# Reordering the node stages between the edge passes of a four-layer graph network: factors before tables, turns before products, a bias added by groups

## The reference, cut to what matters

```python
h = maximum(layernorm(x), 0);  x = x + L0(h)   # attention, W1, batch norm, relu, W2 (+ b2)
h = maximum(layernorm(x), 0);  x = x + L1(h)   # q,k,v = h @ W + b; softmax per target; agg @ Wo + bo
h = maximum(layernorm(x), 0);  x = x + L2(h)   # h @ W, softmax per target of leaky scores
h = maximum(layernorm(x), 0);  x = x + L3(h)   # weighted sum over edges, two products, leaky relu
```

## Time and profile before

| what | value |
|---|---|
| median of 3 runs | 11529.81 us (11526.19 to 11531.22) |
| profiled execution, its own time | 11527.12 us |
| its span, first to last instruction | 11525.4 us |
| busy share of the span: POOL, DVE, ACT, PE | 71%, 63%, 47%, 9% |
| mean granted TensorE clock | 0.517 of full speed |
| stage j1, first product to last table | 4942.5 to 5067.9 us |
| stage j2, first scatter to the head of p2 | 7208.4 to 7289.8 us |

### The profile page before, as it was taken

One profiled execution on the slowest core, in us unless ns is written; L12 is line 12 of the kernel. 1 busy time (PEld: TensorE's weight loads), 2 busy tenths in 40 slices (PEclk: granted clock), 3 DMA queues, 4 the chain that ended last, 5 costly groups with the idle time before them and its releaser, 6 DMA issues.

```text
span 11525.4 us, 40086 instructions
## 1 busy us (share of the span) xinstructions
PE 1039.5 (9%) x4242; PEld 856.6 (7%) x4242; DVE 7232.6 (63%) x7083; ACT 5376.1 (47%) x6139; POOL 8189.6 (71%) x8632
## 2 busy tenths in 40 slices
PE   4122222221000000030000001100000000000001
PEld 3112222221000000020000000100000000000001
DVE  8845555553888888759999997445444543333333
ACT  6144444442666666546666665333333333333332
POOL 2177777777777777657777776777777767777776
PEclk8555555555555555565555555555555555555555
DMA  8756666663666666546666665333333333333333
GB/s 296 264 189 202 204 205 202 201 205 114 215 215 211 213 215 214 183 130 222 225 220 222 224 220 163 85 111 110 113 113 109 112 95 106 103 105 106 106 104 105
DMA packets 793528, 1946.33 MB, mean 169 GB/s; under 512 B 213957, under 2 KB 425885, under 8 KB 792860
## 3 DMA queue, kind: packets, MB, share of 16 engines
q1 hardware_dynamic: 461412, 1129.66, 27.4%
q0 software_dynamic: 331904, 814.65, 25.4%
HBM read 1204.91 MB, written 738.73 MB: 169 GB/s over the span
## 4 chain that ended last, share of the span: by engine, by line
POOL 49%; DVE 22%; issue 20%; DMA 4%; ACT 2%; PE 1%; another core or an unknown queue 1%; DVEq 0%; POOLq 0%; SPq 0%; ACTq 0%
POOL region L1353 47%; DVE work L1498 5%; DVE psB L1403 4%; DMA region<-x,ix_s 2%; DVE psR L1435 2%; DVE work L1431 2%; DVE psR L1491 2%; DVE psR L1483 2%; POOL work L1768 1%; DVE region L645 1%; DVE region L646 1%; PE psB L834 1%; DVE m_ext L1466 0%; POOL start_rows_by_dst L1125 0%
## 5 line engine op out<-in xcount | busy, mean ns | idle before, releaser
L1498 DVE TENSOR_TENSOR_SCAN work<-work,psR 128x1792 f32<-128x1792 f32 (+2 forms) x496 | 1971.1, 3974 | 92.1 <-DVE ix_s L1422 56.1
L1353 POOL DMA_INDIRECT region<-kv,ix_s x1612 | 1525.5, 946 | 497.0 <-issue 494.2
L1353 POOL DMA_INDIRECT region<-x,ix_s x1612 | 1520.9, 944 | 503.0 <-issue 459.6
L1353 POOL DMA_INDIRECT region<-qm,ix_s x1612 | 1523.4, 945 | 492.5 <-issue 489.4
L1353 POOL DMA_INDIRECT region<-h,ix_s x1612 | 1521.2, 944 | 491.3 <-issue 488.9
L1353 POOL DMA_INDIRECT region<-k,ix_s x1612 | 1521.0, 944 | 491.3 <-issue 491.3
L1516 ACT COPY work<-region 128x1664 f32<-128x1664 f32 (+1 forms) x496 | 1162.2, 2343 | 1266.6 <-DMA region<-start_rows_by_dst 735.0
L1403 DVE TENSOR_TENSOR_SCAN psB<-psB,work 128x1792 f32<-128x1792 f32 (+1 forms) x496 | 1485.0, 2994 | 387.1 <-ACT psB L1529 333.7
L1590 ACT COPY work<-work 128x1664 f32<-128x1664 f32 (+2 forms) x496 | 1539.2, 3103 | 0.0
L1589 ACT COPY psR<-work 128x128 f32<-128x128 f32 (+2 forms) x496 | 190.2, 384 | 2728.8 <-DVEq L1499 2728.8
L1431 DVE TENSOR_TENSOR work<-region,psB 128x1664 f32<-128x1664 f32 x372 | 702.1, 1887 | 801.2 <-DMA region<-k,ix_s 528.0
(11 more groups left out here) (330 smaller groups left out, 5060.1 us busy)
## 6 DMA issues: line engine op xcount, KB each, us to landing
region<-start_rows_by_dst SPq DMA_DIRECT2D x248, 832.0 KB, 6.7
state_p<-work SPq DMA_DIRECT2D x124, 936.0 KB, 4.8
state_p<-work SPq DMA_DIRECT2D x124, 884.0 KB, 3.8
region<-start_rows_by_src SPq DMA_DIRECT2D x124, 832.0 KB, 7.4
start_rows_by_dst<-zero_t SPq DMA_DIRECT2D x62, 1664.0 KB, 7.6
state_pA<-work SPq DMA_DIRECT2D x124, 832.0 KB, 4.9
state_p<-work SPq DMA_DIRECT2D x124, 832.0 KB, 3.5
start_rows_by_src<-zero_t SPq DMA_DIRECT2D x1, 59904.0 KB, 163.5
```

Source lines behind the costliest of these rows:

```text
L1353: g_.indirect_dma_start(rows_s[b][:, k, 0:wd_s], None, q.tabs, bass.IndirectOffsetOnAxis(ap=ix_s[b][:, k:k + 1], axis=0))\
L1498: c.do(nc.vector.tensor_tensor_scan(q.st[:, 0:F * (K + 1)], decay_at(q, b)[:, 0:F * (K + 1)], summed[:, 0:F * (K + 1)], 0.0, ALU.mult, ALU ...
```

## The change

In j1 and in j2 a group's factors are made ahead of the table of the group in front of it. PE transposes a group's normalised rows before the next group's W2 product (j1), and in j2 before the table product it also turns the values of the group two further on; `values` and ACT's copy of them run one group further ahead. `bo` is added group by group inside the loop of j1 and no longer at the start of p1.

```diff
-        def proj_pe(pe, nm, w, ncol, g):
+        def proj_turn_pe(pe, nm, g):
             pe.wait_ge(*proj_on(nm, "norm", g + 1))
             pe.wait_ge(*proj_on(nm, "ht", g + 1))
             for j in range(nb(g)):
                 ins = nc.tensor.transpose(psA[:, j * P:(j + 1) * P], hst[:, j, :], ident[:, :])
             ins.then_inc(S("proj_tr"), 1)
+
+        def proj_pe(pe, nm, w, ncol, g):
             pe.wait_ge(*proj_on(nm, "ht", g + 2))
...
-            if q is P1:
-                bias_dve(v, bo_1)
...
+            def group_bias(g):
+
+                xg = blocks(xsb, g)
+                c.do(nc.vector.tensor_tensor(xg, xg, bo_1[:, :].unsqueeze(1).to_broadcast([P, nb(g), D]), ALU.add))
+
             for g in range(NG):
                 add(g)
                 norm_dve(v, "j1", g)
+                factors_dve(v, "j1", g)
+                if g > 1:
+                    group_bias(g - 2)
                 if g:
                     take_dve(v, "j1", 3 * D, g - 1)
-                factors_dve(v, "j1", g)
+            group_bias(NG - 2)
             take_dve(v, "j1", 3 * D, NG - 1)
+            group_bias(NG - 1)
...
             for g in range(NG):
+                proj_turn_pe(pe, "j1", g)
                 if g < NG - 1:
                     second(g + 1)
                 proj_pe(pe, "j1", wcat1[:, :], 3 * D, g)
...
             values(0)
-            for g in range(NG):
-                if g < NG - 1:
-                    values(g + 1)
+            values(1)
+            for g in range(NG):
                 add(g)
                 norm_dve(v, "j2", g)
+                factors_dve(v, "j2", g)
+                if g < NG - 2:
+                    values(g + 2)
                 if g:
                     take_dve(v, "j2", D + 8, g - 1)
-                factors_dve(v, "j2", g)
             take_dve(v, "j2", D + 8, NG - 1)
...
-            def product(g):
+            def turn(g):
                 pe.wait_ge(S("e1_steps"), g * 3 + 3)
                 for j in range(nb(g)):
                     ins = nc.tensor.transpose(psD[:, j * P:(j + 1) * P], vals[:, j, :], ident[:, :])
                 ins.then_inc(S("end_tr"), 1)
+
+            def product(g):
                 pe.wait_ge(S("end_at"), g + 1)
...
+            turn(0)
             product(0)
+            turn(1)
             for g in range(NG):
                 if g < NG - 1:
                     product(g + 1)
+                proj_turn_pe(pe, "j2", g)
+                if g < NG - 2:
+                    turn(g + 2)
                 proj_pe(pe, "j2", w_2[:, :], D + 8, g)
...
             turned(0)
-            for g in range(NG):
-                if g < NG - 1:
-                    turned(g + 1)
+            turned(1)
+            for g in range(NG):
                 proj_act(act, "j2", g)
+                if g < NG - 2:
+                    turned(g + 2)
```

## The result

| | median us | lowest to highest | runs |
|---|---|---|---|
| before | 11526.65 | 11525.63 to 11531.22 | 5 |
| changed | **11467.96** | 11465.29 to 11469.76 | 5 |

The ratio is 0.9946 with an interval of 0.9935 to 0.9958: faster, by 58.7 us. The profiled execution of the changed kernel took 11469.12 us with a span of 11467.4.

The account below looks back on a forecast made before the run. POOL's queue was taken to bound the five passes, so gains lay in the node stages and pass starts: 11527.1 - 34.1 (j1) - 6.2 (bias) - 17.8 (j2) = 11469.0 us. Range given 11457 to 11491, its own 11461 to 11478.

Parts of the forecast that it names:

- The passes: Five passes: bound by POOL's queue, loops untouched; the end moves by whatever time a pass's first gather moves.
- j1, -34.1: Stage j1: period falls from 9.8 to 6.6 us a group, so p1's head gather is issued 34.1 us earlier.
- the ring: In j1: add, factors, normalisation, transposes, next W2 product, add set the period; 6.14 us at high clock, 7.65 low.
- nearer the high end: In j1: period taken as 6.6 us, closer to 6.14 at PE's higher clock level than to 7.65 at the lower.
- The head, -6.2: Start of p1: without DVE's one bias addition the first gather follows the head gather at once, saving 6.2 us.
- Held by something else: Rival at p1's start: not DVE's bias delays the head gather, which stays at 7.14 us; total 11475.2, chance 0.06.
- j2, -17.8: Stage j2: POOL scatters back to back, 5.1 us a group, so p2's head gather comes 17.8 us earlier.
- PE at the lower level, 5.65 us a group: In j2: PE's transposes, table product and Wo product at 1.2 GHz take 5.65 us a group, against POOL's 5.1.
- The signs named: Expected profile: j1 tables about 6.6 us apart, transposes right behind line 834, p1 head 0.98 us, j2 scatters at 1.275 us.
- TensorE at its lower level in j1: Rival in j1: PE stays at the lower clock, 7.65 us a group, gain only 22.7; total 11480.4, chance 0.14.
- the overlap that doesn't form: Rival in j1: transposes keep waiting on ACT or PE, only the bias gain remains; total 11521, chance 0.04.
- the lockstep of 13.4 us a group: Rival in j1: table product waits for the same turn's table, 13.4 us a group; total 11591, chance 0.03.

Follow-up runs that it names:

- the longer normalisation: Changed kernel with one more block of ACT normalisation per group in j1 and j2, into an unread tile: 11473.46 us.
- the longer product: Changed kernel with the table product of one block done twice per group in j1 and j2: 11461.29 us.
- PE's old order: Changed kernel with PE's next W2 product ahead of the transposes again in j1: 11470.69 us, ratio 0.9935.
- the one-input reduction: Changed kernel plus a DVE column sum of xsb with one SBUF input at p1's start, result unread: 11460.32 us, ratio 0.9942.

## Why the prediction was right, step by step

- **The passes**: p1 +0.2 us, the rest -2.4. Moving their first gather moved the end, as said.
- **j1, -34.1 against -36.6.** The mechanism stands: the ring is in the chain, the longer normalisation lengthened it, the longer product didn't. The period at the higher level is 6.19 us (6.14 forecast), at the lower 6.9 to 7.5 (7.65). From the end of the second W2 product to the end of the last, for which the sum has 71.9 us, it took 70.5 (ten periods of 6.50 on the mean and a short one of 5.5), 1.4 less. The last full product took 2.85 us and not the 4.6 taken, 1.75 less. Two small terms were left out: that product waits 0.45 us for ACT's copy, and POOL's part behind the last full table took 6.85 us and not 6.6. The two mis-sized terms are the clock's: "nearer the high end" was not near enough. The Trainium skill (TensorE: Matmul & The Clock Gate, What's actually happening) has the clock follow how busy PE was of late; the rise of 0.78 to 0.89, 1.00 with the longer product and 1.00 in PE's old order agree in direction. By that rule alone the time was to be 6 to 7 us below the sum; j1 came out 2.5 us below it.
- **What the prediction didn't ask**: whether PE's new order in j1 was any good. It found the W2 product in the ring and priced it, but held it only against other rings of the changed order and never against that of PE's order before, in which DVE's 5.27 us are the bound.
- **The head, -6.2 against -6.2.** Right, and shown by three kernels: gone without the addition, moved to the last scatter with it, absent beside the one-input reduction. "Held by something else" (0.06) is out. The Trainium skill (SBUF — State Buffer, Who interferes with whom) infers that a two-input tensor_tensor leaves the making of descriptors alone; 7.14 and 6.76 us against 0.98 and 0.97 say otherwise here. An indirect DMA of this kernel also takes its row numbers from an SBUF tile (`head_i`, `spos`), and no run separates that reading from the making of the descriptors. The bias in the loop is hidden only by slack: four scatters show 1.24 to 1.27 us beside it (one at 4999.88).
- **j2, -17.8 against -18.2.** POOL scattered back to back, as forecast: 61.45 us from the first to the last start, 48 x 1.275 being 61.2, and one scatter at 1.21 us where the sum allowed 1 us in all for such. The step "PE at the lower level, 5.65 us a group" was mis-sized: the clock was 0.72 over the stage, 0.76 in its middle, and no table waited for PE. It made no difference, since POOL was found to be the last either way. Against the old j2 of the other profiles the gain is 11 to 12 us. What the prediction got right is the length of the new stage, 63.5 us against 63.1, which repeats; the difference is near the mark only for the profile it was taken from.
- **The sum.** 11469.0 us against a median of 11467.96 is closer than the terms deserve: in the profiled execution the edited stretches gave 2.9 us more than forecast, and the ones that no edit touches took 3.1 us longer. That they cancel is luck.
- **The signs named.** The tables are 6.4 us apart, the head takes 0.98 us and stands 1.29 us ahead of the first gather, and POOL is idle for at most 0.31 us between two of j2's scatters. One sign was drawn wrongly: the transposes do not stand right behind the table product but wait for the normalisation (1.40, 2.01 and 1.13 us in three turns from 4995 on), as the ring asks.
- **The remaining rivals.** TensorE at its lower level in j1 (7.65 us a group) came in some groups, never in all. Neither the overlap that doesn't form nor the lockstep of 13.4 us a group left a trace.

## What to carry to other kernels

When a software pipeline is reordered, list for each engine's new order which product now stands in which ring, and price the old order of one engine beside the new order of another: here DVE's edit was worth 53 us (133.1 to 79.8 for j1, with the granted clock up from 0.73 to 0.89) and PE's in the same change gave 11 of them back. A long VectorE addition of two SBUF tensors should not stand where GpSimd issues indirect DMAs that the end hangs on; cut it to pieces and place them where GpSimd has slack. The stages whose ring ran through TensorE while its granted clock changed (0.54 to 0.71 over the old j2) had no fixed length (81.3, 75.4, 74.0 us): take the price of such a stage from several profiles before a gain is credited to an edit.

## What was not expected of the hardware

- More work on TensorE made the stage shorter: one product block more per group took the granted clock over j1 from 0.85 to 0.94 and j1 from 91.1 and 92.1 to 89.5 us. It is one profile, and the size is near the spread of j1 in kernels without it (90.1 to 92.2).
- An indirect DMA is held if it starts beside DVE's two-input addition, and by what is left of that: 6.16 us over its usual time with 6.29 to go, 5.7 with 5.83, 5.79 with 5.93. One that started 0.03 us behind the start of a group's addition (5019.17 in the changed kernel) was not held: 0.97 us. A one-input `tensor_scalar` from SBUF to SBUF held one too.
- Two sets of runs differ by 21 us in the kernel before (11526.65, 11547.60) and by 17 in the changed one, with the same ratio, 0.9946.
